# Three units of the next batch ahead of the turn of the first maxima, and the fourth down product behind earlier units

## The reference

```python
x = x + tanh(g_xattn[0]) * L0_xattn(layernorm(x), ctx, ctx)            # softmax(q k / sqrt(8)) v, projections with bias
x = x + tanh(g_ffn[0])   * L0_ffn(layernorm(x))                        # quantised: up, gate, sigmoid, product, down (384 wide)
x = x + tanh(g_xattn[1]) * L1_xattn(layernorm(x), ctx, ctx)            # the same with a causal mask (key > position: -inf)
x = x + tanh(g_ffn[1])   * L1_ffn(layernorm(x))                        # a gated recurrence over the four batches
```

## Time and profile before

| | us |
|---|---|
| median of 3 runs | 335.45 (334.67 to 335.69) |
| profiled execution | 336.59 |
| its span, first to last instruction | 334.6 |
| PE busy | 294.6 (88%) |
| DVE busy | 250.6 (75%) |
| ACT busy | 190.9 (57%) |
| POOL busy | 139.9 (42%) |
| mean granted TensorE clock | 0.974 of 2.4 GHz |

### The profile page before, as it was taken

One profiled execution on the slowest core, in us unless ns is written; L12 is line 12 of the kernel. 1 busy time (PEld: TensorE's weight loads), 2 busy tenths in 40 slices (PEclk: granted clock), 3 DMA queues, 4 the chain that ended last, 5 costly groups with the idle time before them and its releaser, 6 DMA issues. The chain is left out here.

```text
span 334.6 us, 4564 instructions
## 1 busy us (share of the span) xinstructions
PE 294.6 (88%) x1456; PEld 169.4 (51%) x1456; DVE 250.6 (75%) x549; ACT 190.9 (57%) x311; POOL 139.9 (42%) x274
## 2 busy tenths in 40 slices
PE   1789899799989798996997879699989998999994
PEld 1458555455533364442545667574755654434462
DVE  5689877888987379999998895686697692442834
ACT  1672276466476744889899415236566557664232
POOL 6669892752050401684002194921386217141100
PEclk9979999999999999998999997879999999999999
DMA  7920100020000000000000102020002000000004
GB/s 214 357 98 34 71 31 11 0 102 10 1 8 3 0 0 2 1 0 1 0 0 2 69 25 95 2 102 0 10 6 101 4 2 9 0 3 0 1 2 125
DMA packets 9688, 12.57 MB, mean 38 GB/s; under 512 B 896, under 2 KB 5376, under 8 KB 9664
## 3 DMA queue, kind: packets, MB, share of 16 engines
q1 hardware_dynamic: 9232, 11.80, 9.9%
q10 hardware_dynamic: 432, 0.47, 0.7%
HBM read 4.27 MB, written 1.05 MB: 16 GB/s over the span
## 5 line engine op out<-in xcount | busy, mean ns | idle before, releaser
L1425 DVE TENSOR_REDUCE sb_nm<-ps_top 128x3 f32<-128x462 f32 (+2 forms) x168 | 97.7, 626 | 28.1 <-PE ps_top L988 17.9
L787 ACT ACTIVATE sb_pr<-ps_score 128x512 f32<-128x512 f32 (+1 forms) x148 | 81.9, 583 | 56.7 <-PE ps_score L1020 47.5
L988 PE MATMUL ps_top<-sb_Kd,sb_Q 128*128 128x462 f32 (+3 forms) x240 | 71.8, 355 | 4.1 <-DVE sb_nm L1425 3.2
L1020 PE MATMUL ps_score<-sb_Q,sb_Kd 128*128 128x512 f32 x119 | 54.7, 470 | 1.4 <-ACT sb_pr L787 1.0
L988 PEld LDWEIGHTS ps_top<-sb_Kd,sb_Q 128*128 128x128 f32 x240 | 45.1, 195 | 15.8 <-DVE sb_nm L1425 10.5
L1020 PEld LDWEIGHTS ps_score<-sb_Q,sb_Kd 128*128 128x128 f32 x119 | 22.2, 188 | 32.1 <-ACT sb_pr L787 26.7
L641 POOL TENSOR_SCALAR sb_var<-sb_mv 128x4 f32<-128x4 f32 x16 | 3.9, 242 | 75.6 <-DVE sb_mv L1361 75.1
L1052 PE MATMUL ps_pv<-sb_pr,sb_V 128*32 128x512 f32 x256 | 34.1, 605 | 0.0
L635 POOL TENSOR_SCALAR_AFFINE_SELECT sb_pr<-sb_pr 128x512 f32<-128x512 f32 x16 | 10.5, 659 | 43.9 <-ACT sb_pr L787 43.9
L1250 PE MATMUL ps_top<-sb_front,sb_wfT 128*128 128x512 f32 x44 | 22.0, 626 | 1.0 <-ACT sb_u L883 1.0
L643 POOL TENSOR_TENSOR sb_rstd<-sb_var,sb_half 128x4 f32<-128x4 f32 x16 | 19.4, 1211 | 1.3
(11 more groups left out here) (195 smaller groups left out, 556.7 us busy)
## 6 DMA issues: line engine op xcount, KB each, us to landing
sb_Q<-sb_qh SPq DMA_DIRECT2D x16, 256.0 KB, 2.4
sb_Q<-sb_ql SPq DMA_DIRECT2D x8, 256.0 KB, 3.3
sb_xr<-x SPq DMA_DIRECT2D x4, 256.0 KB, 7.2
out<-sb_xr SPq DMA_DIRECT2D x4, 256.0 KB, 2.5
sb_wsb<-w SPq DMA_DIRECT2D x1, 704.0 KB, 8.8
sb_wf<-wffn SPq DMA_DIRECT2D x1, 576.0 KB, 8.4
sb_wkr<-wkr SPq DMA_DIRECT2D x2, 256.0 KB, 6.4
sb_Q<-sb_nmT SPq DMA_DIRECT2D x16, 32.0 KB
```

The source lines that it names most:

```text
L787: act.activation(pr[:, k % PRING, q0:T], score_bank(B * layer + b, t)[:, q0:T], ACT.Exp, scale=SCALE).then_inc(exp_r, 1)
L988: ins = pe.matmul(cols[:, c0:c1, :], Q4[n % 3][:, g, P * qt:P * qt + P], Kd[n % 3][:, g, j:j + c1 - c0, 0:keys], start=True, stop=not mask ...
L1020: ins = pe.matmul(ps[:, :], Kd[n % 3][:, g, j, 0:P], Q4[n % 3][:, g, :], start=True, stop=True, skip_group_check=True)
L1425: dve.tensor_reduce(nm[:, :, :].rearrange("p t h -> p (t h)")[:, f0:f0 + heads], top[k % MRING][:, 0:keys * heads].rearrange("p (h k) -> p ...
```

## The change

First, in stage -1 units 0, 1 and 2 of batch 1 move from slots 15 and 16 to slot 14. There PE issues them, then the five filling matmuls (which move from slot 13 to slot 14, behind them), then the turn of batch 0's maxima. The other five of the eight early units come one in each of slots 15 to 19. The order on DVE stays: last maximum of batch 0, split, maxima of batch 1. Second, since PE may now finish units of batch 1 before the split has been turned, `nm` gets two buffers, taken by the batch's number. Third, parts 0 and 1 of the fourth down product come behind unit 7, part 2 behind unit 9. No instruction is added or removed.

```diff
-LAST_DOWN_AT = (11, 12, 13)
+LAST_DOWN_AT = {7: (0, 1), 9: (2,)}
...
-    if slot >= SLOTS - EARLY and 0 < i + 2 < B:
+    if i == -1 and slot == LAST + 1:
+        taken += [(1, u) for u in range(MRING)]
+    elif i == -1 and slot > LAST + 1:
+        k, n = slot - LAST - 2, FIRST_EARLY - MRING
+        taken += [(1, MRING + u) for u in range(n * k // EARLY, n * (k + 1) // EARLY)]
+    elif slot >= SLOTS - EARLY and 0 < i + 2 < B:
...
-        nm = sb("nm", [P, TT, H])
+        nm = sb("nm", [P, 2, TT, H])
...
-                            if (layer, i, b) == (1, -1, 0) and u in LAST_DOWN_AT:
-                                down(B - 1, LAST_DOWN_AT.index(u))
+                            if (layer, i, b) == (1, -1, 0):
+                                for m in LAST_DOWN_AT.get(u, ()):
+                                    down(B - 1, m)
...
-                        if i == -1 and slot == LAST:
+                        if i == -1 and slot == LAST + 1:
                             fill(5)
...
-                dve.tensor_reduce(nm[:, :, :].rearrange("p t h -> p (t h)")[:, f0:f0 + heads],
+                dve.tensor_reduce(nm[:, b % 2, :, :].rearrange("p t h -> p (t h)")[:, f0:f0 + heads],
...
-                src = nm[:, :, :].rearrange("p t (g j) -> p t j g", g=G)
+                src = nm[:, b % 2, :, :].rearrange("p t (g j) -> p t j g", g=G)
```

## The result

| | before | after |
|---|---|---|
| median, us | 335.21 (333.51 to 335.71, 7 runs) | 333.25 (331.65 to 336.68, 7 runs) |
| ratio | | 0.9942, 95% interval 0.9916 to 0.9969 |
| profiled execution, span | 336.59, 334.6 | 333.80, 331.8 |
| mean granted clock in it | 0.974 | 0.982 |

The changed kernel is 0.6% faster, 2.0 us between the medians, where 4.1 were forecast. The ratio leaves out executions that are over 1.5% above the kernel's fastest; the 336.68 is one.

A forecast was written before the change was run, and what follows sets the result against it. PE was taken as the bound, with time to gain in its waits in layer 1's stage -1. Layer 1's -4.3 us and layer 0's +0.2 gave -4.1, against the 335.45 median: 331.4 us, range 330.1 to 334.1.

The forecast's parts named there:

- The bound and its place: Whole kernel: PE bounds it, busy 88% of the span; the time to be had lies in PE's waits in layer 1's stage -1.
- Parts 0 and 1 in the wait of unit 8: Layer 1: two down-product parts fill 2.0 us of PE's idle time ahead of unit 8, at a cost of 0.1 us.
- Part 2 and the units behind it: Layer 1: part 2 adds 1.0 us, full clock saves 1.5; last maximum at 212.8 instead of 214.26, 1.4 us earlier.
- The split: Layer 1, DVE behind the last maximum: 0.8 us (0.55 to 1.4) where it was 1.5, possibly meeting POOL's `q_low`.
- Turn to tile: Layer 1: 1.23 us from turn to end of copy, 3.0 to the transfer's landing; first tile waits for it, by 0.7.
- The turn of batch 2: Layer 1's stage -1: waits for DVE's `q_low` and moves from 206.41 to 206.0; no PE gap longer than 1.3 us.
- Layer 0, the turn 0.2 us late: Layer 0: unit 2 and five fills delay the turn and first tile by 0.2 us (0 to 0.5).
- the 4.3 us: Layer 1: first tile at 218.1 instead of 222.39, a gain of 4.3 us passed on in full.
- The first rival: Half clock behind the transfer waits ahead of the first tiles, 1.3 us a layer: 332.7 or, both layers, 334.0; chance 0.24.
- the turn is held up more: Rival: units and fills delay the turn, 0.5 us in layer 0 and 1.3 more in layer 1: 333.0; chance 0.13.
- Not passed on: Rival: something behind the first tile, such as POOL's masks or batch 2's query transfers, decides: 335.4; chance 0.06.
- Slower: Rival: half clock through 6 us of both layers' tile stages, losing 2 x 3.0 us: 337.4; chance 0.07.

The follow-up runs named there:

- e6: Kernel e1 with POOL's residual additions ahead of the low part of batch 2's queries in layer 1's stage -1: 332.02 us, ratio 0.9921 to before.
- e1: Changed kernel with units and fills moved ahead of the turn in layer 1 only, down products still moved: 331.71 us, ratio 0.9917 to before.
- e3: Kernel before with only the down products moved; units, fills and turn as before: 332.72 us, ratio 0.9934.
- e4: Full changed kernel plus nine unread filling matmuls in layer 0's wait for the transfer: 331.92 us, ratio 0.9923 to before.
- e8: Kernel e6 with the five fills back ahead of the three units, as in the kernel before: 331.18 us, ratio 0.9905 to before.
- e9: The changed kernel run again, unedited: 332.79 us, ratio 0.9954 to before.
- e11: Kernel e8 plus seven unread filling matmuls in layer 1's wait for the transfer: 331.28 us, ratio 0.9900 to before.
- e2: Changed kernel with the down products put back where they were, units moved in both layers: 335.12 us, ratio 1.0019 to before.
- e5: Kernel before with units and fills moved ahead of the turn in layer 0 only, down products as before: 335.12 us, ratio 1.0003.
- e7: Kernel before, nothing moved, with unread filling matmuls added in PE's two idle times in layer 1: 332.98 us, ratio 0.9956.

## Why the prediction was right or wrong

**The bound and its place**: right. PE's waits in stage -1 of layer 1 were what there was to be had, and what was saved there passed on in full. Most of it was the clock behind the waits and not the time in them.

**Parts 0 and 1 in the wait of unit 8**: right. They took 2.02 us, unit 8 came 6.33 us behind the first unit, as before (6.32), and the clock stayed at 1.00 to 206.

**Part 2 and the units behind it**: the direction was right, two terms were too large. Unit 10's maximum was put at 10.15 us behind the first unit, and came at 9.92; the last maximum was put at 19.0 and came at 18.2. Unit 12's maximum came 0.3 us earlier than said; the eight maxima follow one another at 0.55 us and not at 0.6 (four take 2.28 us from 208.29), and the 0.4 us left for the projection of batch 2's queries were 0.2. This is the low bound that the prediction had for "no wait is left", 2.2 us.

**The split**: mis-sized. 0.8 us was taken, 1.53 measured; the upper end of 1.4 was passed. The cause was named, but given the smaller value: the trace shows POOL's `q_low` from 213.50 to 214.78 and DVE's first instruction ending at 214.86, and e6 took it away (1.12 to 0.29 us). In layer 1's split each of the two DVE instructions ends 0.07 to 0.08 us behind the POOL instruction that was running when it began, before, after and in e6. The Trainium skill, page "SBUF — State Buffer", section "Who interferes with whom", says that the engine that issues first keeps the shared ports for its whole instruction and the other blocks fully; these ends agree with that, and the 0.6 us that the prediction set aside for it were nearer than my value. It hid behind unit 2 and the fills: the turn came only 0.2 us later than these allowed. That the tile came within 0.3 us of the forecast is therefore partly luck: units 0.8 us faster and a split 0.7 us slower than forecast nearly cancel.

**Turn to tile**: 1.24 us to the end of the copy and 2.88 to the tile, against 1.23 and 3.0. Right, and the tile waits for the transfer by 0.66 us (0.7 forecast).

**The turn of batch 2**: it came at 207.41, 11.9 us behind the first unit (12.2 forecast), but PE now waits 1.54 us for it where it waited 0.47:

```profile
207.41 0.63 PE L970 MATMUL ps_misc<-sb_consts,sb_xn 128*128 128x128 f32 x4 [1.54 <-DVE sb_ql L1422]
```

The prediction's "no gap is longer than 1.3 us" overlooked this one. The clock did not fall behind it, here or in the seven other traces with this order (e1, e3, e4, e6, e8, e9, e11).

**Layer 0, the turn 0.2 us late**: 0.29. Right.

**Where it went wrong: what the 4.3 us are measured against.** The sum was made from one profile of before, in which the clock was at half from 201 and from 215 to 221.8, and was then taken off the median. The prediction gave full clock afterwards, but never asked whether before's other executions had these stretches. The profiled one was 1.1 us over the median, and that was mentioned and set aside. At full clock layer 1's tile is at 25.4, not 28.6: the moves are worth 1.4 us there. The last sentence of the sum is the step that failed; its total was right to 0.3 us in layer 1 for the execution that it came from. That the range holds the result is luck as far as this step goes: its upper end was there for the first two rivals, and most of the missing gain has a reason that none of them names (e1, which is free of the first, still lacks 1.5 us).

**The first rival** came true in part: in the profiled execution the clock fell behind layer 0's wait (priced at 1.3 us; the first `weigh` shows 1.0, all of layer 0 in e2 against e3 1.7), not behind layer 1's. With the wait filled it did not fall in e4's trace; e5 and e9 show that it does not fall in each execution with the wait. It is not a cause of the whole gap: e1, free of it, is at 0.9917, a gain of 2.8 us and not of 4.3. One and the same kernel took from 332.0 to 338.1 us with clocks from 1.000 to 0.972. The Trainium skill, page "TensorE: Matmul & The Clock Gate", Part 1, says that the window in which the chip judges TensorE's activity is free-running and does not reset when a kernel starts. That would explain why the same wait is followed by half clock in one execution and not in another; the runs agree with it as far as their spread goes, but none shows where the window stood.

**The other rivals.** That the turn is held up more: not so (0.29 and 0.0 us). Not passed on: excluded by 112.3 us behind the tile. Slower, by half clock in both layers' tile stages: no profile shows it. One of nineteen executions of the changed kernel (336.68 us, mean clock 0.972) had much half clock, but seven of the 88 of the kernel before had the same 0.972, and where it lay isn't known.

**Open**: how often the clock falls behind each wait. The profiles show one execution each, and the mean clock of the others doesn't say where it was lost. The feed-forward part has a stretch of its own near 156 in eight of the thirteen traces, 3.4 or 6.8 us, in code that no kernel here touched: with the longer one layer 0 took 1.3 us more (e7 against e3). What of the medians' differences comes from there isn't known.

## What to carry to other kernels

A wait of PE is priced twice: by what lies in it, and by the clock behind it; before moving work into it, fill it with matmuls that nobody reads, and see how much of the gain that alone brings (here as much as the change: 0.9956 against 0.9942 and 0.9954). Make the sum against executions at the same granted clock, and when the one profile lies above the median, ask which of its waits the others don't have. Work pulled ahead of a step on the path empties the wait behind that step: in layer 0, where the transfer decided, it could only cost.

## What the runs showed of the hardware

Behind a wait of 1.3 us ahead of layer 0's first tile came a stretch at half clock in one execution of the changed kernel (at 40) and none in another (e9). Behind 2.6 us ahead of layer 1's turn came one in before and none in e3 and e5, and behind 1.54 us ahead of batch 2's turn none in any of eight traces. So the length of the wait alone does not decide. The two DVE instructions of the split, both on 64 numbers a partition, took 0.71 and 0.73 us beside POOL's copies of keys (before), 1.11 and 0.39 beside its `q_low` (after), and 0.22 and 0.27 with POOL idle (before, at 232.97): their time depends on which POOL instruction they meet, and moving POOL's long one by 1.7 us took 0.8 us off the split.
